# A second feed-forward part's first group by seven products, and the seam in front of it

## What is computed

```python
x = x + 0.5 * _L0_ffn_ref(_layernorm(x, axis=-1), L0_ffn_W_up, L0_ffn_W_gate, L0_ffn_W_down)
x = x + _L0_attn_ref(_layernorm(x, axis=-1), L0_attn_W_in, ...)   # the state-space part
x = x + 0.5 * _L0_ffn_ref(_layernorm(x, axis=-1), L0_ffn_W_up, L0_ffn_W_gate, L0_ffn_W_down)
# _L0_ffn_ref: wu, wg, wd = ternary_quant(W_up), ternary_quant(W_gate), ternary_quant(W_down)
up = jnp.einsum('bsd,ed->bse', x, wu)
gate = jnp.einsum('bsd,ed->bse', x, wg)
hidden = jax.nn.silu(up) * gate
return jnp.einsum('bse,de->bsd', hidden, wd)
```

## Time and profile before

| | |
|---|---|
| median of 3 runs | 1777.09 us (1776.42 to 1780.38) |
| profiled execution, its time | 1778.58 us |
| its span | 1776.8 us |
| PE busy | 1748.5 us, 98% |
| DVE, ACT, POOL busy | 1339.8, 943.1, 823.5 us |
| granted TensorE clock | 0.999 of full speed |
| blocks | f1 to about 630 us, state-space to 1174, f2 to the end |

### The profile page before, as it was taken

The page is one execution under the profiler, slowest core; times in us unless marked ns, Lnnn a source line. Parts: engine busy times, 40 slices in busy tenths (PEclk is TensorE's granted clock), DMA queues, the critical chain, the costliest instruction groups (busy, mean ns, idle before and its releaser), DMA issues. The chain is left out here.

```text
span 1776.8 us, 35778 instructions
## 1 busy us (share of the span) xinstructions
PE 1748.5 (98%) x13280; PEld 1288.3 (73%) x13280; DVE 1339.8 (75%) x2317; ACT 943.1 (53%) x1421; POOL 823.5 (46%) x565
## 2 busy tenths in 40 slices
PE   7999999999999999999999999999999999999999
PEld 4588888888888844544444444555888888888888
DVE  7988777887776758778777777657887777877655
ACT  7744746457464465545445536334547465474653
POOL 2766436244362426446456456625245263352533
PEclk9999999999999999999999999999999999999999
DMA  7032131111312031112112112012121311112100
GB/s 331 25 90 43 47 89 29 60 42 47 89 35 108 0 104 34 63 36 62 56 35 68 56 36 69 30 65 43 48 43 47 89 42 48 42 48 65 42 24 24
DMA packets 125196, 104.49 MB, mean 59 GB/s; under 512 B 104000, under 2 KB 104512, under 8 KB 119744
## 3 DMA queue, kind: packets, MB, share of 16 engines
q1 hardware_dynamic: 125120, 103.60, 19.1%
HBM read 49.59 MB, written 25.17 MB: 42 GB/s over the span
## 5 line engine op out<-in xcount | busy, mean ns | idle before, releaser
L504 POOL TENSOR_TENSOR f_hlo<-f_h,f_hhi 128x768 f16<-128x768 f32 x135 | 201.9, 1496 | 598.2 <-ACT f_hhi L687 569.3
L1261 PE MATMUL f_gate_ps<-spare 128*128 128x256 f16 x2688 | 329.8, 272 | 0.2
L1185 PE MATMUL f_down_ps<-wd,f_hhi 128*128 128x256 fp8e4 x1440 | 318.4, 273 | 0.7 <-DVE xa L882 0.7
L1185 PE MATMUL f_down_ps<-wd,f_hlo 128*128 128x256 fp8e4 x1440 | 318.4, 273 | 0.0
L1261 PEld LDWEIGHTS f_gate_ps<-spare 128*128 128x128 fp8e4 x2688 | 254.8, 97 | 45.2 <-issue 1.9
L1261 PE MATMUL f_up_ps<-spare,wu 128*128 128x256 f16 x1792 | 229.9, 273 | 0.1
L1261 PEld LDWEIGHTS f_up_ps<-spare,wu 128*128 128x128 fp8e4 x1792 | 172.8, 98 | 23.3 <-issue 0.7
L882 DVE SCALAR_TENSOR_TENSOR xa<-f_down_ps,out_scale,xa 128x512 f32<-128x512 f32 x195 | 136.3, 742 | 59.2 <-PE f_down_ps L1185 58.9
L1647 POOL TENSOR_TENSOR s_am<-s_tri,s_al 128x512 f16<-128x512 f16 x128 | 155.1, 1242 | 21.5 <-DVE s_al L1919 18.8
L1185 PEld LDWEIGHTS f_down_ps<-wd,f_hhi 128*128 128x128 f16 x1440 | 140.9, 98 | 17.9 <-issue 1.6
L1185 PEld LDWEIGHTS f_down_ps<-wd,f_hlo 128*128 128x128 f16 x1440 | 140.9, 98 | 16.2
(11 more groups left out here) (247 smaller groups left out, 3296.6 us busy)
## 6 DMA issues: line engine op xcount, KB each, us to landing
xa<-res SPq DMA_DIRECT2D x16, 1024.0 KB, 5.4
res<-xa SPq DMA_DIRECT2D x15, 1024.0 KB, 3.9
res<-xa SPq DMA_DIRECT2D x34, 256.0 KB, 2.0
xa<-in_u SPq DMA_DIRECT2D x8, 1024.0 KB, 4.8
xa<-res SPq DMA_DIRECT2D x32, 256.0 KB, 2.6
late<-in_w_gate SPq DMA_DIRECT2D x4, 1024.0 KB, 17.1
...
```

The lines of the kernel that those rows point to most:

```text
L504: last = nc.gpsimd.tensor_tensor(hlo[:, p, a:b, :], src, hhi[:, p, a:b, :], ALU.subtract)
L1185: last = nc.tensor.matmul(at, part[:, p, kind, m * P:(m + 1) * P], wd[:, weight, p, :], start=(p == 0 and part is hhi and (m == 0 or name ...
L1261: last = nc.tensor.matmul(acc[:, j * HT:(j + 1) * HT], w[:, k, e * P:(e + 1) * P], xop[part][:, o, k, :, :], start=(fresh and (j, k, part) ...
```

## The change

f2's group 0 goes by seven products too (NC is 0 in f2). Its seven operands are made in the last state-space group: ACT normalizes the rows (`normalize_behind`, an Identity activation with a scale and a bias per row that carry the factor XS) and rounds the high parts into memory that sequence 0 no longer uses; DVE makes T1 to T4 (`behind_sums`) and the low parts (`low_behind`); SP turns both (`turn_behind`), the high part when ACT is done, the low part when DVE is. The 16 transposes, `high_parts` and `low_parts` of the seam go. `inv_std` of this group moves ahead in POOL's chunk 1. The output projection of chunk 2 is cut in two halves, one before the transposes of x and one after y; that of chunk 3 writes to another bank (`s_turn`) from another buffer (`yv_last` in `spare`), so that it need not wait for the residual before. The last chunk's store is issued by f2's SP rather than in the state-space block, and the loads of f2's groups 1 and 2 follow it one after the other.

Group 1's operands are made during f2's group 0, inside the pairs: DVE takes statistics in pairs 1 and 2, the variance in 2, scale and bias in 3 (the statistics of group 2 stay in 3 and 4, its variance in 5), T1 and T3 in 6, T2 and T4 in 7; ACT normalizes in pairs 4 and 5 and rounds in 6, 7 and after; POOL makes the four low parts, one after `low_parts` of pair 6 and three after those of pair 7. Their transposes wait for P4 of group 0's pair 7, since they write the same `xst`. Group 2 is prepared during `down`, as in any other group. f1 is unchanged.

```diff
-                NC = 1
+                NC = 1 if first else 0
...
-                            load(2, out_p)
+                            sp.dma_start(out_v[:, CH * NG - 1:CH * NG, :], xa[:, 0, CH - 1, :]).then_inc(chunks_out, 16)
                             sp.wait_ge(chunks_out, 16 * CH * NG)
                             load(1, out_p)
+                            sp.wait_ge(x_in, 16)
+                            load(2, out_p)
...
+                        def second_low(i):
+                            pool.wait_ge(second_high, i + 1)
+                            lo, of = (row_groups(xn, second_diffs, rows[1][n])[i] for n in (1, 0))
+                            last = nc.gpsimd.tensor_tensor(lo[0], lo[1], of[0], ALU.subtract)
+                            if i == 3:
+                                last.then_inc(rl_done, 2)
...
+                                if second and p > 5:
+                                    for i in {6: (0,), 7: (1, 2, 3)}[p]:
+                                        second_low(i)
...
+                        def normalize_second(c):
+                            act.wait_ge(par_step, 2)
+                            nc.scalar.activation(xn[:, c, :], xa[:, slot(1), c, :], ACT.Identity, bias=second_par[:, 1, c:c + 1],
+                                                 scale=second_par[:, 0, c:c + 1]).then_inc(second_normal, 1)
+                        def high_second(i):
+                            if i == 0:
+                                act.wait_ge(second_normal, CH)
+                            elif i > 1:
+                                act.wait_ge(second_sum, 2 * i - 2)
+                            dst, of = row_groups(xn, second_diffs, rows[1][0])[i]
+                            last = nc.scalar.activation(dst, of, ACT.Copy)
+                            last.then_inc(second_high, 1)
+                            if i == 3:
+                                act.sem_inc(rh_done, 6)
...
+                                if not first and g == 0:
+                                    for c in {4: (0, 1), 5: (2, 3)}.get(p, ()):
+                                        normalize_second(c)
+                                    for i in {6: (0,), 7: (1, 2)}.get(p, ()):
+                                        high_second(i)
...
+                            B11, B21, B12, B22, T1, T3, T2, T4 = row_parts(xn, second_diffs)
+                            if p in (1, 2):
+                                stats(1, 2 * p - 2)
+                                stats(1, 2 * p - 1)
+                            if p == 2:
+                                dve.wait_ge(stat_done, after(2 * CH))
+                                variance(1)
+                            if p == 3:
+                                dve.wait_ge(rstd_done, after(2))
+                                nc.vector.tensor_scalar(second_par[:, 0, :], rstd[:, :], XS, None, ALU.mult).then_inc(par_step, 1)
+                                dve.wait_ge(par_step, 1)
+                                nc.vector.scalar_tensor_tensor(second_par[:, 1, :], mv[:, :, 0], -1.0, second_par[:, 0, :],
+                                                               ALU.mult, ALU.mult).then_inc(par_step, 1)
+                            if p == 6:
+                                dve.wait_ge(second_normal, CH)
+                                nc.vector.tensor_tensor(T1, B12, B11, ALU.subtract).then_inc(second_sum, 1)
+                                nc.vector.tensor_tensor(T3, B22, B12, ALU.subtract).then_inc(second_sum, 1)
+                            if p == 7:
+                                dve.wait_ge(second_sum, 1)
+                                nc.vector.tensor_tensor(T2, B22, T1, ALU.subtract).then_inc(second_sum, 1)
+                                dve.wait_ge(second_sum, 3)
+                                nc.vector.tensor_tensor(T4, B21, T2, ALU.subtract).then_inc(second_sum, 1)
...
                             n = pair_of(g, p)
-                            if p == 0:
-                                pe.wait_ge(st_turned, 32 * (g - NC + 1))
+                            if p == 0 and fresh:
+                                pe.wait_ge(rows_turned, 32)
+                            elif p == 0:
+                                pe.wait_ge(st_turned, turned_at(g))
                                 pe.wait_ge(res_done, res_at(g - 1, STEPS[ORDER.index("P3")]))
-                            pe.wait_ge(sil_done, after(KE * g + 2 * p - 3 if p > 1 else KE * g))
+                            if p or not fresh:
+                                pe.wait_ge(sil_done, after(KE * g + 2 * p - 3 if p > 1 else KE * g))
...
+                        def turn_behind(part):
+                            sp.wait_ge((behind_high, behind_low)[part], 4)
+                            sp.dma_start_transpose(spare[:, 4096 + 1792 * part:4096 + 1792 * (part + 1)].bitcast(F16)
+                                                   .rearrange("p (n t) -> p n t", t=P), behind_at[part].bitcast(F16))\
+                              .then_inc(rows_turned, 16)
...
+                                if g is LAST and c == 2:
+                                    turn_behind(0)
+                                    turn_behind(1)
...
+                            for c in range(CH):
+                                nc.scalar.activation(xn[:, c, :], xa[:, 2, c, :], ACT.Identity, bias=behind_par[:, 1, c:c + 1],
+                                                     scale=behind_par[:, 0, c:c + 1]).then_inc(behind_normal, 1)
+                        def high_behind(i):
+                            if i == 0:
+                                act.wait_ge(behind_normal, CH)
+                                act.wait_ge(y4_done, after(CH * order(LAST)))
+                            elif i > 1:
+                                act.wait_ge(behind_sum, 2 * i - 2)
+                            dst, of = row_groups(xn, behind_diffs, behind_split[0])[i]
+                            nc.scalar.activation(dst, of, ACT.Copy).then_inc(behind_high, 1)
...
+                                    if c == 1:
+                                        normalize_behind()
+                                        high_behind(0)
+                                    if c == 2:
+                                        for i in range(1, 4):
+                                            high_behind(i)
...
+                        def behind_scale():
+                            dve.wait_ge(rstd_done, after(order(BEHIND) + 1))
+                            nc.vector.tensor_scalar(behind_par[:, 0, :], rstd[:, :], XS, None, ALU.mult).then_inc(par_step, 1)
+                            dve.wait_ge(par_step, 1)
+                            nc.vector.scalar_tensor_tensor(behind_par[:, 1, :], mv[:, :, 0], -1.0, behind_par[:, 0, :],
+                                                           ALU.mult, ALU.mult).then_inc(par_step, 1)
+                        def behind_sums(part):
+                            B11, B21, B12, B22, T1, T3, T2, T4 = row_parts(xn, behind_diffs)
+                            if part == 0:
+                                dve.wait_ge(behind_normal, CH)
+                                nc.vector.tensor_tensor(T1, B12, B11, ALU.subtract).then_inc(behind_sum, 1)
+                                nc.vector.tensor_tensor(T3, B22, B12, ALU.subtract).then_inc(behind_sum, 1)
+                            else:
+                                dve.wait_ge(behind_sum, 1)
+                                nc.vector.tensor_tensor(T2, B22, T1, ALU.subtract).then_inc(behind_sum, 1)
+                                dve.wait_ge(behind_sum, 3)
+                                nc.vector.tensor_tensor(T4, B21, T2, ALU.subtract).then_inc(behind_sum, 1)
+                        def low_behind(i):
+                            dve.wait_ge(behind_high, i + 1)
+                            lo, of = (row_groups(xn, behind_diffs, behind_split[n])[i] for n in (1, 0))
+                            nc.vector.tensor_tensor(lo[0], lo[1], of[0], ALU.subtract).then_inc(behind_low, 1)
...
+                                if c and ahead is BEHIND:
+                                    (behind_scale, lambda: low_behind(0), lambda: low_behind(2))[c - 1]()
...
-                                    normalize(ahead, 0, CH // 2)
+                                    behind_sums(1)
+                                if c == 3 and ahead is BEHIND:
+                                    low_behind(3)
...
+                                    if ahead is BEHIND:
+                                        dve.wait_ge(stat_done, after(CH * order(ahead) + CH))
+                                        variance(ahead)
+                                if c == 1 and ahead is BEHIND:
+                                    behind_sums(0)
+                                if c == 2 and ahead is BEHIND:
+                                    low_behind(1)
...
+                                if last_chunk(g, c):
```

(8 more changed lines are left out.)

246 lines of the change are left out of this document (109 added, 137 removed).

## The result

| | before | changed |
|---|---|---|
| median | 1778.68 us (8 runs) | 1784.86 us (8 runs) |
| ratio changed / before | | 1.0036 (95%: 1.0026 to 1.0045) |
| span of the profiled execution | 1776.8 us | 1783.4 us |
| f2's first matmul | 1175.68 | 1173.82 |
| P1 of f2's group 1 | 1256.57 | 1263.51 |

A forecast was written before the change was run, and what follows sets the result against it. TensorE, nearly alone, was taken to bound f2. The terms −7.13 + 7.5 + 0.8 + 0 − 0.6 − 0.3 gave +0.3 us on a median of 1777.09, so 1777.4 us, range 1770.5 to 1781.

The forecast's parts named there:

- The pitch: f2's group 0: seven products take 73.76 us where the direct group takes 80.89, so −7.13.
- The stalls in the pairs: Group 0's pairs: group 1's preparation exceeds engine slack and is blocked beside POOL, stalling TensorE by +7.5 us (2.4 to 9.1).
- Group 1's operands and what stands behind them: Behind P2 of `down`: operands land just in time, 19.8 against 19.87 us; DVE's later group 2 work included, +0.8.
- the high one is through by then: Group 1's transposes: the high part's is finished before the low part's, leaving one 3.6 us issue and 5.2 to landing.
- Group 1's own excess: f2's two groups behind the first: the 0.32 us over twice the pitch goes, −0.3.
- The seam: Before f2: about 1.1 us won by moved projections and removed transposes is given back by blocked DVE operations; 0 (−1.8 to +0.5).
- The end of the block: Border to f2: the last store's 0.33 us issue and its wait leave the path, −0.6 (−1.1 to 0).
- B: Faster rival: DVE wins the turn between POOL's low parts, group 0 stalls by 2.4 us; 1771.0 us, chance 0.32.
- C: Slower rival: POOL's last low part comes late, so group 1's P1 waits for the transpose; 1781.5 us, chance 0.15.

The follow-up runs named there:

- e6: e2 with only T1 to T4 moved to either side of `up_sum` in pairs 6 and 7: 1776.95 us, ratio 0.9989 to the kernel before.
- e7: e2 with all of group 1's preparation steps moved within group 0's pairs, and two low parts of group 0 moved behind `dtx`: 1776.54 us, ratio 0.9987.
- e8: e7 with scale, bias, T1 to T4 and POOL's first low part of group 1 placed anew: 1773.26 us, ratio 0.9969.
- e2: e1 with the transpose of group 1's high parts issued before the low parts are ready: 1778.50 us, ratio 0.9997.
- e4: The changed kernel without POOL's four low parts of group 1, set to zero once instead: 1778.39 us, ratio 0.9996.
- e1: The changed kernel with group 2's wait for POOL's last low part moved from the first preparation step to the third: 1778.92 us, ratio 1.0001.
- e9: The kernel before with only the last store issued behind the border and the loads one after the other: 1778.06 us, ratio 0.9991.

## Why the prediction was wrong, point by point

**The pitch, −7.13.** Groups by seven products keep their 73.76; that term stands. Group 0 takes 80.77 in e6, 81.34 in e7 and 78.24 in e8, against 80.89 directly: only e8 keeps a part of it that counts, 2.65.

**The stalls in the pairs, +7.5.** Measured 7.94. The starts of `up_sum` are 6.16 apart where nothing stalls, and 7.37, 6.78, 7.53, 7.01 and 8.35 in pairs 2 to 6:

| pair | forecast | measured | |
|---|---|---|---|
| 1 | 0 | 0 | the statistics hide |
| 2 | 0.4 | 1.21 | the variance's addition is blocked too |
| 3 | 1.55 | 0.62 | the scale is blocked for 1.35, the bias not |
| 4 | 0.6 | 1.37 | 1.33 of it is TensorE standing inside a product, where it waits for neither ACT nor DVE as far as the profile shows |
| 5 | 0.85 | 0.85 | |
| 6 | 2.2 | 2.19 | T1 and T3 blocked, and 0.85 of TensorE standing beside it |
| 7 | 1.9 | 1.56 | T4 blocked, but by another operation |
| ahead of pair 0 | 0 | 0.14 | |

The sum was good, to a large part by luck. Pair 5 is right, by its mechanism too (TensorE waits 0.69 for ACT's copy). In pair 4 the size fell to something that the forecast has no term for; e2, e4, e6 and e8 show the same, a stall of 0.81, 0.81, 0.82 and 1.25 with 0.78, 0.78, 0.79 and 1.21 of standing in it, so nothing is seen of ACT's two normalizations. In pair 6 DVE's `hidden_first` ends at 1225.98 and TensorE's product behind its 0.85 at 1226.05, so that either would have given nearly the whole size; e6, with the T's no longer blocked, keeps 1.24. A T that is not blocked takes 0.68 there, not the 0.55 of the forecast. In pair 7 the size is nearly right and its reason wrong, as e4 showed. In pairs 2 and 3 I had only counted operations with two SBUF inputs as blocked; these rows show otherwise:

```profile
1193.96 1.04 DVE L854 TENSOR_SCALAR f_var<-f_mv 128x4 f32<-128x4 f32 x1
...
1200.21 1.35 DVE L920 TENSOR_SCALAR second_par<-f_rstd 128x4 f32<-128x4 f32 x1
1201.60 0.16 DVE L922 SCALAR_TENSOR_TENSOR second_par<-f_mv,second_par 128x4 f32<-128x4 f32 x1
...
1214.32 0.27 DVE L854 TENSOR_SCALAR f_var<-f_mv 128x4 f32<-128x4 f32 x1
```

```profile
1192.85 2.13 POOL L542 TENSOR_TENSOR f_hlo<-spare,f_hhi 128x1024 f16<-128x1024 f32 x1
...
1199.41 2.13 POOL L542 TENSOR_TENSOR f_hlo<-late,f_hhi 128x1024 f16<-128x1024 f32 x1
```

The variance's addition (L854) and the scale (L920) have one tensor input and 4 columns, and end within 0.03 us of POOL's low parts (1194.98 and 1201.54); the same L854 takes 0.27 in pair 5. The bias, with two inputs, comes when POOL is through, and takes 0.16.

**Group 1's operands and what stands behind them, +0.8 (0 to 3).** This is the step that failed. It measured 7.99. I had asked when the operands are ready for TensorE, and for that question the estimate was fair: POOL was done 10.1 us after P2 of `down` (11 forecast), and without the rest the transposes would have cost 1.43 (e1). I had written in one clause that DVE's preparation of group 2 and its additions "come later too", and gave it a part of 0.8. But that preparation waits for the same POOL operation, it stands first in DVE's queue, and the additions that empty TensorE's banks stand behind it. I had followed the operands, and not what is queued behind the step. With the numbers of this trace it comes out: POOL's end at 10.1 after P2, the step's 1.3 and four additions of 2.7 together give 14.1; TensorE had run out of banks at 1245.20, which is 9.55 after P2. That is 4.6 us of idle time (4.75 measured), and with the forecast's own 11 it would have been 5.5. The clock then adds its part: the 36 matmuls of the stretch take 6.85 us, where they would take 3.92 at the usual 0.109 apiece: 2.9. With the 4.75 that is 7.7 of the 7.99.

The second error is smaller: "the high one is through by then". SP waits for both parts before it issues either, as the code says, so that the first issue lies on the path as well (e2 takes it off).

**Group 1's own excess, −0.3.** The two groups behind the first take 147.75, which is still 0.23 over twice 73.76, where 0.32 was to go: −0.09.

**The seam, 0.** f2 starts at 1173.82, 1.86 sooner than in the earlier trace rows. But the trace of the kernel before holds some 1.6 us from a stretch at the lower clock, which I had not noticed; without it f2 would start there at 1174.1 (e9, without such a stretch and with 0.53 less at the border, has 1173.61, which fits). So seam and border together gave 0.3, and since the border gave 0.99 of it, the seam itself cost 0.7: just past the bound of +0.5. The give and take inside is as described: TensorE waits 0.30 and 1.01 for `s_cd` and 0.96 before y, and e7 takes 1.07 of this back by moving two of DVE's low parts.

**The end of the block, −0.6.** Measured −0.99 (1.46 to 0.47), of which the store is 0.53.

**The rivals.** B did not come in the changed kernel; an order of the steps that comes near it exists (e8, with 4.48 of stalls in group 0 where B had 2.4), but had to be looked for. C had the right side and the wrong mechanism: its price was the DMA's, 3 us, and its point ("later than 11 us") was not reached. The range ended at 1781 since no case held a wait of DVE with the additions behind it.
